# Attention with heads on one core: output weights loaded in the attention's own block, and the first batch's low keys and queries between the flag and the jump

## The reference

```python
q = layernorm(x) @ wq + bq;  k = ctx @ wk + bk;  v = ctx @ wv + bv
x = x + softmax(heads(q) . heads(k) / sqrt(8)) @ heads(v) @ wo + bo
```

## Time and profile before

| | us |
|---|---|
| median of 3 runs | 2539.92 (2537.13 to 2540.59) |
| profiled execution, its own time | 2547.37 |
| its span, on which all rows below stand | 2545.6 |
| granted TensorE clock, mean over the span | 0.916 |
| ACT busy in the span | 1454.1 |
| DVE busy in the span | 1288.3 |
| POOL busy in the span | 237.9 |

### The profile page before, as it was taken

The page is one execution under the profiler, slowest core; times in us unless marked ns, Lnnn a source line. Parts: engine busy times, 40 slices in busy tenths (PEclk is TensorE's granted clock), DMA queues, the critical chain, the costliest instruction groups (busy, mean ns, idle before and its releaser), DMA issues. The chain is left out here.

```text
span 2545.6 us, 45852 instructions
## 1 busy us (share of the span) xinstructions
PE 2148.0 (84%) x18128; PEld 1496.1 (59%) x18128; DVE 1288.3 (51%) x1666; ACT 1454.1 (57%) x1758; POOL 237.9 (9%) x305
## 2 busy tenths in 40 slices
PE   4767978979789469999748999979966999976998
PEld 2544855747558246666435666647744666655886
DVE  4552342334333566666557777743236666643111
ACT  2334445454454458888637888852235888872332
POOL 1005023140230400000010000010010000000000
PEclk9997989989889789999869999978987999996999
DMA  5758336354463568888046788620034887720000
GB/s 182 230 171 294 149 136 238 113 197 181 148 219 113 162 142 186 187 187 186 17 111 153 186 187 187 158 61 1 0 79 109 184 188 187 186 65 1 26 17 21
DMA packets 119703, 352.73 MB, mean 139 GB/s; under 512 B 20122, under 2 KB 54800, under 8 KB 118896
## 3 DMA queue, kind: packets, MB, share of 16 engines
q1 hardware_dynamic: 105728, 322.40, 46.6%
q0 software_dynamic: 13776, 27.54, 3.7%
HBM read 257.58 MB, written 91.23 MB: 137 GB/s over the span
## 5 line engine op out<-in xcount | busy, mean ns | idle before, releaser
L947 ACT ACTIVATE a_probs<-a_score 128x1200 f32<-128x1200 f32 x768 | 858.0, 1169 | 202.5 <-PE a_score L860 202.3
L860 PE MATMUL a_score<-a_qstack,a_kstack 128*128 128x400 f32 x2304 | 552.0, 371 | 56.9 <-DVE a_qstack L1030 56.0
L860 PEld LDWEIGHTS a_score<-a_qstack,a_kstack 128*128 128x128 f32 x2304 | 379.3, 190 | 227.3 <-issue 178.9
L822 PE MATMUL a_numer<-a_probs,a_v 128*18 128x200 f32 (+1 forms) x9216 | 470.2, 334 | 0.0
L822 PEld LDWEIGHTS a_numer<-a_probs,a_v 128*18 128x18 f32 (+1 forms) x9216 | 228.1, 97 | 183.7 <-issue 87.7
L1021 DVE TENSOR_TENSOR a_kstack<-a_kraw,a_kstack 64x2888 fp32r<-64x2888 f32 x90 | 284.8, 3165 | 2.8
L1030 DVE TENSOR_TENSOR a_qstack<-a_qrep,k_groupmask 128x1600 fp32r<-128x1600 f32 x48 | 87.6, 1826 | 172.3 <-PE a_score L860 143.1
L1016 DVE CAST a_kstack<-a_kraw 128x2888 fp32r<-128x2888 f32 x90 | 149.9, 1665 | 10.7 <-DVE a_own L1081 9.3
L1487 ACT ACTIVATE f3d_hidden<-f3d_ph,f_b 128x400 f32<-128x400 f32 x128 | 76.1, 594 | 117.3 <-PE f3d_ph L1445 110.0
L1697 PEld LDWEIGHTS f0r_ph<-f0r_xsT,f0r_w 128*128 128x128 f32 x896 | 118.8, 198 | 30.5 <-issue 12.5
L1697 PE MATMUL f0r_ph<-f0r_xsT,f0r_w 128*128 128x128 f32 x896 | 122.6, 281 | 9.3 <-DVE f0r_xsT L1878 9.3
(11 more groups left out here) (360 smaller groups left out, 2782.8 us busy)
## 6 DMA issues: line engine op xcount, KB each, us to landing
a_kraw<-keys SPq DMA_DIRECT2D x384, 361.0 KB, 6.2
values<-kv_vst SPq DMA_DIRECT2D x32, 1296.0 KB
a_v<-values SPq DMA_DIRECT2D x48, 864.0 KB, 5.8
keys<-kv_made SPq DMA_DIRECT2D x48, 722.0 KB
l0a_ctxT<-in_ctxT SPq DMA_DIRECT2D x16, 722.0 KB, 6.4
kv_ctxT<-in_ctxT SPq DMA_DIRECT2D x16, 722.0 KB, 6.6
l0a_ctx<-in_ctx SPq DMA_DIRECT2D x16, 704.0 KB
l0a_mask<-in_mask_BxSxS_ik SPq DMA_DIRECT2D x16, 564.1 KB
```

Source lines behind the costliest of these rows:

```text
L822: last = pe.matmul(numer[32 * g:32 * g + PC, p * 2 * SQ:(p + 1) * 2 * SQ], v[0:rows(t), j, t, (2 * g + p) * PC:(2 * g + p + 1) * PC], prob ...
L860: last = pe.matmul(to, kstack[:, j, g * SK + t * 128:g * SK + (t + 1) * 128], qstack[:, j, g * GH:(g + 1) * GH, :], start=True, stop=not s ...
L947: act.activation(probs[:, n % NP, :].rearrange("p (g q) -> p g q", g=SPAN), slot_ps[:, n % 2, :, 0:GQ], ACT.Exp, scale=HSCALE).then_inc(ex ...
```

## The change

The 16 loads of `wo2` move from POOL's list in the layernorm's block to a list of its own in the attention's block. On DVE, the low keys of batch 0 move from ahead of the bound to behind the flag, the queries of batch 0 (and in round 2 the masking of its values) move out of the jump's target to ahead of the jump, and the order is now low keys of half 0, queries, low keys of half 1, masking, jump.

```diff
-            for h in range(H):
-                g, p, j = h // GH, h % GH // 2, h % 2
-                at = 32 * g + (HD + 1) * j
-                pool.dma_start(wo2[at:at + HD, p, :], ins[f"wo{layer}"][h * HD:(h + 1) * HD, :]).then_inc(wo_in, 16)
             for n in range(2):
                 pool.tensor_copy(stack[:, n, :, :].rearrange("p g (r m c) -> p g r m c", r=2, m=2)[:, :, :, n, :],
...
         KHALF = GROUPS // 2 * SK
+
+        @block.gpsimd
+        def _(pool):
+            for h in range(H):
+                g, p, j = h // GH, h % GH // 2, h % 2
+                at = 32 * g + (HD + 1) * j
+                pool.dma_start(wo2[at:at + HD, p, :], ins[f"wo{layer}"][h * HD:(h + 1) * HD, :]).then_inc(wo_in, 16)
...
-            for half in range(2):
-                dve.wait_ge(k_high, half + 1)
-                low = kstack[64:128, 0, half * KHALF:(half + 1) * KHALF]
-                dve.tensor_tensor(low, kraw[64:128, half, :], low.bitcast(F32), ALU.subtract).then_inc(k_low, 1)
             dve.wait_ge(bound_full, 1)
...
                 numer_ = numer[:, 0:GQ].rearrange("r (p j q) -> r p j q", p=PAIRS, j=2)
-                block_queries(0)
-                if masked:
-                    mask_values(0)
...
+            for half in range(2):
+                low_keys(0, half)
+                if half == 0:
+                    block_queries(0)
+            if masked:
+                mask_values(0)
             dve.wait_ge(numer_free, 1)
             dve.wait_ge(flag_ready, 1)
             dve.sem_inc(parted, 1)
```

## The result

The changed kernel takes 2499.09 us (median of 4 runs, 2498.48 to 2501.22), where the kernel before takes 2538.53 us in the same comparison (4 runs, 2537.02 to 2540.59). The ratio is 0.9846, with a 95% interval of 0.9829 to 0.9863: 39.4 us faster.

The account below looks back on a forecast made before the run. ACT's exponentials pace the unchanged batch loop, so only the three attention starts count. Part 1's 8.5 plus part 2's (DVE's order) 15.2 gave 23.7 us: 2523.7 profiled, 2516.2 median; range 2503 to 2526.

Parts of the forecast that it names:

- given back in batches 0 and 1: Attention start: part of PE's earlier first score is lost again, as PE waits for batch 1's keys from DVE.
- part 1: Layernorm's end: moving the `wo2` loads frees the barrier, so keys and queries are ready earlier; 8.5 us over three layers.
- DVE's jump now starts at E: DVE at the flag: E, the end of low keys, queries, low keys, is M + 9.4; the jump follows, 9.75 us.
- M: Attention start: the end of PE's bound matmuls, from which the flag's timing is counted; 893.67 in layer 1 before.
- The disputed price: Behind the flag: how much the jump's length depends on load; DVE's was taken as the present 9.4 to 9.75 us.
- My lower bound of 4.5 us: DVE's jump: its estimated length without any wait for the keys; the upper estimate was 12 us.
- The 0.35 us: Jump's instruction fetch: waits for one packet of keys under round-robin DMA rings, so most of 6.4 us would be fixed.
- The short jump: Rival, chance 0.20: DVE's jump falls below 6.3 us, PE never waits for batch 1; 35.7 us won, 2504.
- The barrier: Layernorm's end: forecast to fall to 0.70 us; rival, chance 0.08: it stays, part 1 gives nothing, 2525.
- lag to catch up with: Rival, chance 0.05: late DVE delays loads, PE waits in 45 later batches; slower, 2561 at 1 us a batch.
- my 1 us for the landing: Second half of the keys: estimated time added after its last bytes leave, 0 to 1.3 possible.
- The clock term of layer 1: Query stage, `qlow` to `qrep`: a longer pause in PE's matmuls lowers its clock, charged 1.0 us.

Follow-up runs that it names:

- experiment 3: The changed kernel (third kernel run) with DVE's sequencer held ahead of the flag until its low keys, and in round 2 the masking, are finished; 2519.68 us, ratio 0.9887.
- experiment 4: The kernel before, with SP loading the keys of batch 1 only once DVE is past its jump; 2534.72 us, ratio 0.9943.
- the fifth kernel: The changed kernel run again, nothing further altered, on another chip; 2499.87 us, ratio 0.9852.
- the eighth: The changed kernel, with ACT copying the second half of batch 0's keys only after its last `qrep`; 2485.43 us, ratio 0.9793.
- the sixth: The changed kernel, with SP loading the keys of batch 1 only after PE's first slot of scores; 2504.02 us, ratio 0.9865.

## Why the prediction was wrong

By its own terms, from the profiled executions (us, layers 1, 2 and 3):

| term | forecast | measured |
|---|---|---|
| second key copy ends earlier | 3.9, 2.7, 2.0 | 4.9, 3.8, 3.4 |
| query stage, from that copy to the last `qrep` | -1.0, +0.9, 0 | -0.6, +1.8, +0.8 |
| PE's idle time before its first score | 9.2, 8.9, 9.1 | 9.20, 8.87, 9.06 |
| given back in batches 0 and 1 | -3.5, -5.1, -3.4 | -0.4, -0.4, -4.4 |
| sum | 23.7 | 36.0 |

Of the 12.3 us between the two sums, 6.8 are in the row of what is given back and 5.6 in the two rows of part 1.

**The step that failed** is "DVE's jump now starts at E and not at the flag", and with it "everything DVE does for batch 1 stands behind it". It took the sequencer and the engine of DVE for one. The jump is the sequencer's work. It needs the flag and not the engine, so it starts at M + 2.1 (881.1 less 879.02), runs under the 7.5 us of work that its engine has ahead, and costs nothing. That this is the cause is shown: with the sequencer held (experiment 3) the hole of 8.6 to 9.2 us and waits for batch 1 appear, and 8 to 9 us of gain go. What is given back there, worked out as in the table, is 2.3, 7.8 and 2.1 us, 12.2 in all where I had forecast 12.0. The total agrees in part by luck, for I had it split 3.5, 5.1 and 3.4. It was to be read before as well: in the earlier trace rows the hole has the releaser "issue", a hint that it belongs to the sequencer, and I didn't ask what the sequencer would do with a full engine queue. The Trainium skill, "Perfetto Trace Analysis", DVE / Act Engine Instruction, says that the sequencer pushes an instruction into a wait queue and is then ready for the next; the rows of L1109 and L1066 agree.

**The disputed price** came out at the short end. I took 9.4 to 9.75 us for DVE's jump. On either engine a jump is 3.3 to 4.0 us without key loads and 8.6 to 9.75 with them, shown from both sides: in the old order with the keys held (experiment 4) and in the new one with the jump pushed under the keys (experiment 3). In the new order both jumps are taken 2 us before the first low keys let SP load, so neither meets a load. My lower bound of 4.5 us was even too high. PE's jump does not keep its 9.3 us with nothing moving, so most of it is not fixed. The 0.35 us for which I let a fetch wait behind the keys doesn't hold either: the runs show about 6 us. The Trainium skill, "DMA: Bandwidth & Descriptors", Queues, rings and completion order, has a DMA engine drain a whole packet from one ring before it turns to the next, and a packet there holds typically 9 to 17 descriptors. I had taken one packet of the profile for such a packet. If it is a single descriptor, the rule gives an estimate of 3.1 to 5.9 us (0.35 times 9 to 17), near the 6 measured. No run here tells which it is, so why it takes 6 us behind the keys stays open.

**The rivals.** The short jump gave 35.7 us and 2504, and the three stretches did fall by 35.9. That its number fits is luck: 35.7 was 8.5 for part 1 and 27.2 for part 2, and the table has 14.1 and 21.9. Its mechanism fits only in part: the request did not get in between the two halves' loads but ahead of both, and DVE's jump would have been hidden at 7 us as well. The barrier went to 0.72 us as forecast, so that rival falls, though the keys seem to have a share in how long POOL's drain was; and DVE has no lag to catch up with.

**Part 1** had the right mechanism. Two terms were too small, and by 5.6 us together, which alone would have carried the time from the short jump's 2504 out of the range. The keys are there about 1 us earlier in each layer than I worked out from the rate step and my 1 us for the landing (the second copy starts the moment they land), 3.5 us in all. Nearly all of that is a term I had put at nothing. I let the keys go at their old pace, and they go faster: the rate steps up at about 864.0, 1281.0 and 1860.0 us, which is 19.6, 19.1 and 20.1 us after the layernorm's start where it was 20.4, 20.1 and 21.7. It fits that POOL's packets no longer go beside them. The second copy starts 0.7 to 1.1 us after that step, so the 1 us for the landing was about right. (My bound of 1.3 us for it doesn't follow from the 877.43 that I gave, which is the start of the first half's copy.) And the query stage won about 1 us in layers 2 and 3 that I had not charged. The clock term of layer 1 was right in kind: the granted clock from first `qlow` to last `qrep` there is 0.73 where it was 1.00. A window of the changed kernel over that stage:

```profile
869.21:878.54 9.33, 8.62 (x53) 8.44 (x54) 8.46 (x15) 5.18 (x11) 0.00 (x0) 0.73 0.01 2
```

**Not foreseen: layer 3's batch 0.** It takes 24.5 us from the first exponential to that of batch 1, before 20.1; in layers 1 and 2 it is 20.7 and 20.5 (before 20.3 and 20.1). PE stops for 1.93 us after five score matmuls and then runs at half clock for longer. Windows of the changed kernel, columns as in the earlier trace rows:

```profile
1890.00:1895.00 5.00, 2.85 (x9) 2.09 (x7) 4.41 (x3) 2.35 (x3) 0.00 (x0) 0.50 1.03 212
1895.00:1900.00 5.00, 4.96 (x25) 3.15 (x25) 4.16 (x2) 3.00 (x3) 0.00 (x0) 0.50 0.78 166
1900.00:1905.00 5.00, 5.00 (x58) 2.96 (x57) 4.39 (x2) 3.66 (x4) 0.00 (x0) 0.84 0.95 228
```

The granted clock is 0.50, its lower level of 1.2 GHz, until about 1900. The same hole is 1.36 us in the fifth kernel, where batch 0 takes 22.8 us, 1.47 us in the eighth with 22.0, and absent in the sixth and the third, with 21.8 and 22.3. So some 2 us are lost in this layer without any hole, and of the 4.4 us how much is the hole and how much the clock behind it stays open.

## What to carry to other kernels

A jump or a flag that an engine's sequencer reads costs its engine nothing if enough work is queued ahead of it and the sequencer is not held by a wait of its own: make the flag first, queue the work that doesn't depend on it, then jump. Take the jump before large loads start: here 3.5 us became 9 behind a load. And small DMAs of GpSimd held the end of a block by its drain for 8 to 10 us, while the same from SyncE cost the barrier at most 1.7 us of issuing: issue them elsewhere, and then look for the wait that comes to light behind the barrier, which here was worth another 14 us.

## What the runs showed of the hardware

- The same taken branch costs PE 3.3 to 3.9 us and DVE 3.7 to 4.0 us (experiment 4) when no keys are moving, and 9.2 to 9.7 us (PE) and 8.6 to 9.75 us (DVE) while key loads hold the DMA engines.
- DVE's sequencer read a flag and branched 7.5 us ahead of the end of its engine's work, with one instruction running there and two queued, and in the masked round with three queued (its L1066 starts right behind the masking, at 1307.34).
- GpSimd's drain at the end of the layernorm takes 12.3 to 13.8 us behind 16 of its own 4 KB DMAs while keys load, and 1.8 us where the same DMAs are SyncE's. Behind the same 16 in the attention's block of the changed kernel it takes 6.5 to 7.3 us.
- Beside the key loads the packets of GpSimd's DMAs move at 43 a microsecond, about one for each of the keys' (86 and 90 in 2 us), and at some 170 where hardly any others are left (339 in 2 us).
